# One partition maximum for the keys of all images, behind the last image

## What is computed

```python
xf = x.reshape(b, n, d)
keys = xf @ Wk.T
softmax_keys = jax.nn.softmax(keys, axis=1)
values = _bn(xf @ Wv.T, gamma_v, beta_v, axes=(0, 2), ch_shape=(1, -1, 1))
queries = _bn(queries, gamma_q, beta_q, axes=(0, 2, 3), ch_shape=(1, -1, 1, 1))
content_lambda = jnp.einsum('bmk,bmv->bkv', softmax_keys, values)
position_lambdas = jnp.einsum('nmk,bmv->bnkv', E, values)
content_output = jnp.einsum('bknh,bkv->bhvn', queries, content_lambda)
position_output = jnp.einsum('bknh,bnkv->bhvn', queries, position_lambdas)
return (content_output + position_output).reshape(b, d, n1, n2)
```

## Time and profile before

| | |
|---|---|
| median of 3 runs | 1595.41 us (1594.87 to 1595.89) |
| profiled execution | 1599.93 us, span 1598.2 us |
| TensorE busy | 1483.3 us, 93% of the span |
| VectorE busy | 1016.7 us, 64% |
| GpSimd busy | 675.6 us, 42% |
| ScalarE busy | 427.5 us, 27% |

### The profile page before, as it was taken

One profiled execution on the slowest core, in us unless ns is written; L12 is line 12 of the kernel. 1 busy time (PEld: TensorE's weight loads), 2 busy tenths in 40 slices (PEclk: granted clock), 3 DMA queues, 4 the chain that ended last, 5 costly groups with the idle time before them and its releaser, 6 DMA issues.

```text
span 1598.2 us, 27819 instructions
## 1 busy us (share of the span) xinstructions
PE 1483.3 (93%) x10407; PEld 1243.3 (78%) x10407; DVE 1016.7 (64%) x1496; ACT 427.5 (27%) x738; POOL 675.6 (42%) x453
## 2 busy tenths in 40 slices
PE   6765368999999999999999999999999999999997
PEld 6655247888888888888888888888888888888886
DVE  6645597666666666666666666666666666666663
ACT  4435432222222222222222222222222222222220
POOL 4333525444444444444444444444444444444441
PEclk9878689999999999999999999999999999999999
DMA  6453142233343434241525243333434251525221
GB/s 227 170 192 112 15 65 60 60 90 68 74 85 85 85 85 86 60 92 45 112 59 112 59 103 67 78 67 85 85 85 85 76 95 47 92 58 112 59 52 27
DMA packets 338460, 134.68 MB, mean 84 GB/s; under 512 B 202640, under 2 KB 333824, under 8 KB 337920
## 3 DMA queue, kind: packets, MB, share of 16 engines
q1 hardware_dynamic: 338432, 134.31, 36.7%
HBM read 109.12 MB, written 25.17 MB: 84 GB/s over the span
## 4 chain that ended last, share of the span: by engine, by line
PE 87%; issue 5%; DVE 3%; POOL 3%; ACT 1%; DMA 0%; DVEq 0%; SPq 0%; POOLq 0%; ACTq 0%
PE ps_a L989 76%; PE ps_b L1008 8%; PE ps_b L919 2%; POOL x_in L398 1%; PE ps_a L909 1%; POOL keys L405 1%; DVE e_lo L679 1%; POOL key_top L403 0%; DVE b_lo L691 0%; DVE bn L639 0%; PE ps_b L950 0%; DVE q_stats L671 0%; DMA x_in<-in_x 0%; DVE t_lo L691 0%; ACT x_t L500 0%
## 5 line engine op out<-in xcount | busy, mean ns | idle before, releaser
L989 PE MATMUL ps_a<-v_hi,e_hi 128*128 128x512 f32 x1792 | 706.0, 394 | 12.8 <-issue 12.1
L989 PE MATMUL ps_a<-v_hi,e_lo 128*128 128x512 f32 x1792 | 699.0, 390 | 0.0
L989 PEld LDWEIGHTS ps_a<-v_hi,e_hi 128*128 128x128 f32 x1792 | 337.1, 188 | 86.6 <-issue 12.9
L989 PE MATMUL ps_a<-b_lo,e_hi 128*128 128x512 f32 x1024 | 399.2, 390 | 2.6 <-DVE b_lo L691 2.6
L989 PEld LDWEIGHTS ps_a<-v_hi,e_lo 128*128 128x128 f32 x1792 | 337.3, 188 | 68.2
L525 ACT ACTIVATE e_hi<-e_nat 128x512 fp32r<-128x512 f32 x320 | 202.1, 632 | 603.4 <-PE ps_a L989 598.3
L437 POOL TENSOR_TENSOR q_diag<-qn,row_mask 128x1024 f32<-128x1024 f32 x128 | 249.1, 1967 | 222.4 <-PE ps_b L1008 208.2
L433 POOL TENSOR_TENSOR e_nat<-e_nat,s_buf 128x512 f32<-128x512 f32 x64 | 83.5, 1305 | 553.3 <-DVE e_lo L679 553.3
L679 DVE TENSOR_TENSOR e_lo<-e_nat,e_hi 128x512 fp32r<-128x512 f32 x320 | 301.1, 941 | 2.0 <-ACT e_hi L525 0.3
L989 PE MATMUL ps_a<-t_lo,e_hi 128*128 128x512 f32 x768 | 300.0, 391 | 0.0
L752 DVE TENSOR_TENSOR pos<-ps_a,content 128x512 f32<-128x512 f32 x189 | 130.7, 692 | 178.4 <-PE ps_a L989 175.9
(11 more groups left out here) (107 smaller groups left out, 758.5 us busy)
## 6 DMA issues: line engine op xcount, KB each, us to landing
e_nat<-in_L_conv_E SPq DMA_DIRECT2D x128, 512.0 KB, 4.8
x_in<-in_x SPq DMA_DIRECT2D x32, 512.0 KB, 4.2
res<-in_x SPq DMA_DIRECT2D x64, 256.0 KB, 6.8
out_dram<-res SPq DMA_DIRECT2D x64, 256.0 KB, 4.9
q_dram<-q_nat SPq DMA_DIRECT2D x4, 2048.0 KB, 7.6
q_blk<-q_dram SPq DMA_DIRECT2D x32, 256.0 KB, 5.4
gam_q<-in_L_conv_gamma_q SPq DMA_DIRECT2D x8, 0.1 KB, 4.9
bet_q<-in_L_conv_beta_q SPq DMA_DIRECT2D x8, 0.1 KB, 4.6
```

Source lines behind the costliest of these rows:

```text
L989: ins = nc.tensor.matmul(BANK_OF[i], e[:, i, j].rearrange("p n k -> p (n k)"), v[:, j], start=(STARTS[i] and j == 0 and n == 0), stop=(STO ...
```

## The change

key_max and key_top become four times as large and hold all quarters. The buffers move to regions that are free at that time (over content and q_blk), so SyncE waits for keys_shifted before it loads q_blk. keys_max(a) no longer waits for the subtraction, only for the one before it of its own kind. GpSimd does one maximum over 512 columns, when all four key_max are there, and then four subtractions, four exponentials are done by ScalarE, and four sums by GpSimd. e_sums moves ahead of the maximum.

```diff
@@ buffers
         top_level = sb("top_level", [P, J // 2, G, KD], stack=early)
+        key_top = sb("key_top", [P, A, G, KD], stack=early)
...
         v_stats = sb("v_stats", [P, J, A, 6], stack=early)
+        key_max = sb("key_max", [P, A, G, KD], stack=early)
...
-        key_max = sb("key_max", [P, G, KD], stack=early)
-        key_top = sb("key_top", [P, G, KD], stack=early)
@@ SyncE
             sp.wait_ge(v_var_ready, 1)
+            sp.wait_ge(keys_shifted, 1)
             load_q(0, 0)
             load_q(1, 1)
@@ GpSimd
+            def reduce_keys():
+                pool.wait_ge(key_max_ready, A)
+                link(pool.partition_all_reduce(key_top[:].rearrange("p a g k -> p (a g k)"),
+                                               key_max[:].rearrange("p a g k -> p (a g k)"), P, RMAX))
+
             def shift_keys(a):
-                pool.wait_ge(key_max_ready, a + 1)
-                link(pool.partition_all_reduce(key_top[:].rearrange("p g k -> p (g k)"),
-                                               key_max[:].rearrange("p g k -> p (g k)"), P, RMAX))
-                pool.tensor_tensor(keys[:, :, :, a], keys[:, :, :, a], key_top[:].unsqueeze(1).to_broadcast([P, J, G, KD]),
+                pool.tensor_tensor(keys[:, :, :, a], keys[:, :, :, a], key_top[:, a].unsqueeze(1).to_broadcast([P, J, G, KD]),
                                    ALU.subtract).then_inc(keys_shifted, 1)
...
             for k in range(len(BATCHES)):
                 norm_images(k)
-                if k == 4:
-                    shift_keys(0)
-                if k == 6:
-                    shift_keys(1)
+            e_sums(0, 0, 32, first=True)
+            reduce_keys()
+            for a in range(A):
+                shift_keys(a)
             sum_keys(0)
-            e_sums(0, 0, 32, first=True)
-            shift_keys(2)
             sum_keys(1)
-            shift_keys(3)
@@ ScalarE
                 read_proj(8 * a + G - 1, a, G - 1, a % QS)
-                if a == 2:
-                    exp_keys(0)
-                if a == 3:
-                    exp_keys(1)
-                    exp_keys(2)
-
...
-            exp_keys(3)
+            for a in range(A):
+                exp_keys(a)
             value_split_hi(0)
@@ VectorE
             def keys_max(a):
                 dve.wait_ge(proj_read, 8 * a + 8)
                 if a > 0:
-                    dve.wait_ge(keys_shifted, a)
+                    dve.wait_ge(key_max_ready, a)
...
-                nc.vector.tensor_tensor(key_max[:], top_level[:, 0], top_level[:, 1], ALU.max).then_inc(key_max_ready, 1)
+                nc.vector.tensor_tensor(key_max[:, a], top_level[:, 0], top_level[:, 1], ALU.max).then_inc(key_max_ready, 1)
```

## The result

The changed kernel takes 1556.78 us (median of 4 runs, 1556.22 to 1557.45), against 1595.65 for the kernel before in the same comparison (4 runs, 1594.87 to 1597.36). The ratio is 0.9755, 95% interval 0.9738 to 0.9772. That is 38.9 us less, where 34.7 was forecast, and inside the range of 1551 to 1574. The profiled execution took 1557.23 us for a span of 1555.5, which is 42.7 us less than the profiled one before. The two differences disagree by 3.8 us, because the profiled execution of before (1599.93) was 4.3 us above the median of this comparison, and this one is 0.45 above its own. In every comparison the executions of the kernel before spread from about 1595 to 1600; what parts them was not found.

The account below looks back on a forecast made before the run. The opening was taken as a serial path whose last wait at each place is GpSimd. 35.5 + 10.4 - 10.2 - 1.0 = 34.7 us, so 1595.4 becomes 1560.7 us; the range holding 8 in 10 is 1551 to 1574.

Parts of the forecast that it names:

- Part 1: Between the images: without two partition maxima the last gn_bias comes at 96.6 instead of 132.1, a gain of 35.5 us.
- Part 2: Last gn_bias to last key maximum: VectorE's 8.78 us wait goes and its maxima take 1.4 us, a gain of 10.4 us.
- Part 3: Last key maximum to last subtraction: three more subtractions (6.9 us) and a longer partition maximum (3.3 us), a loss of 10.2 us.
- The forecast's signs for this part: After the last key maximum, M: the partition maximum's record some 6 us later, the first subtraction at about M + 21.3.
- The growth by the columns: Extra time of one partition maximum of 512 columns over one of 128: 3.3 us, between bounds 0 and 6.6.
- Part 4: Behind the last subtraction: all four sums of exponentials, then L461, come later; price 1 us, bounds -1.5 and +5.
- the 19 forecast: The sums of exponentials on GpSimd are ready near 19 us behind the last subtraction.
- (C): Opening: images don't keep the pace as loads, stores and statistics meet; 16 us a group, 9 us more, 1570; chance 6%.
- (A): Partition maximum grows with its columns at 4.94 us: growth 14.8 instead of 3.3, 1572.2 us; chance 8%.
- (D): Slower than before: the long maximum's cost per column eats the gain, from 0.099 us a column; chance 3%.
- (B): Serial tail: sums of quarters 0 and 1 and L461 land on the path, 9.9 us instead of 1.0, 1569.6; chance 8%.

Follow-up runs that it names:

- spread statistics: The changed kernel with VectorE's statistics spread evenly between the groups of images, some moved behind the last group: 1553.61 us, ratio 0.973.
- kernel with the fill: The changed kernel with a fill of one element per partition, waiting for the last key maximum, put directly ahead of the partition maximum: 1564.04 us, ratio 0.9787.
- doubled maximum: The changed kernel with its partition maximum of 512 columns done twice in a row, same input and output: 1559.6 us, ratio 0.9757.
- kernels without a maximum: The changed kernel with the partition maximum replaced by an ordinary GpSimd fill of key_top with zeros, subtractions kept: 1553.94 us, ratio 0.9725.
- VectorE's subtractions: The changed kernel with the four key subtractions on VectorE, behind its normalisation of the values, instead of on GpSimd: 1553.54 us, ratio 0.9718.

## Why the prediction was right

The sign, the place and the range were right: 34.7 us against 38.9 in the medians and 42.7 in the profiles. That the sum came so near is partly luck, since one of its four steps failed and another was too large. By its own steps, which are counted in the profiles:

- **Part 1**, 35.5 us: measured 31.8 (132.06 to 100.24). The mechanism holds, and the size was off by 3.7. One gap of four images was 13.1 as taken, but the first took 14.0 (59.06 to 73.05), and the last 14.05 instead of 11.2. The step took 13.1 and 11.2 from gaps that have neither of two things, and a gap of 14.0 has both (11.2 + 1.6 + 1.2). The first is the clock: after a wait of 1.90 us for VectorE, the eight transposes of the next image take 1.95 us instead of 1.07 and its projection 2.69 instead of 1.94; the granted clock is 0.60 from 57 to 60 us, so most of it went at the lower of the clock's two levels, 1.2 GHz in place of 2.4. The same kernel, run again, has the same wait of 1.90 us at 57.53 and a granted clock of 1.00 behind it, and that gap is 12.7 us (59.09 to 71.76); so the fall doesn't come every time. The second is TensorE's wait of 1.18 us for ScalarE's copy at the turn of a quarter, which stands in both gaps of 14.0. So in the last gap VectorE's lateness, the only thing the step took off, wasn't the bound: VectorE waited 6.40 us for the average there. In before both lay in the gaps with the maxima, which the step replaced whole. The spread statistics, which take away the wait for VectorE, got the last gn_bias 6.0 us sooner.
- **Part 2**, 10.4 us: measured 132.23 to 163.88 against 100.40 to 121.61, a gain of 10.4. The maxima took 1.4 us, as taken.
- **Part 3**, a loss of 10.2 us: measured none. From the last key maximum to the end of the last subtraction it is 20.2 us before and after (121.61 to 141.80). This is the step that failed: it says that "the same stretch has the same VectorE work beside it" and takes over the 5.97 us until the record and the 4.94 us in it. The 5.97 us were read as a cost that stands behind M; they begin where GpSimd's last sum ends (163.74), 0.14 us ahead of M, so the row couldn't tell which of the two set the start. But the loading starts as soon as GpSimd has nothing ordinary left to do, ahead of the wait, and then the maximum is over before VectorE's long two-input operations begin (123.56 against 127.63). Each is shown: with the loading held back (the kernel with the fill), both come back and the first subtraction moves from 9.0 to 19.1 us behind the last key maximum. The forecast's signs for this part failed: the record follows 0.14 us behind M, not some 6, and the first subtraction 9.0 us behind it, not 21.3. So 5.7 us of loading and 3.1 us of the record went (1.81 instead of 4.94), and the subtractions cost 8.8 us more (11.15 instead of 2.31), which comes to nothing. The growth by the columns, 3.3 us in the sum, was 1.1, shown by the doubled maximum. The rule of the Trainium skill (Perfetto Trace Analysis, GPSIMD Engine Instruction) to go by spacings of starts gives the same as the record if two maxima in a row are taken (1.91 us against 1.80). What misled was the spacing to the next ordinary instruction, which contains the loading back. The four subtractions took 11.15 us instead of 9.2, since the first met VectorE's last t_raw (130.44 to 132.73).
- **Part 4**, a loss of 1 us: measured 25.2 instead of 24.3 us to the first evacuation, 0.9. The size is right, but partly by chance. VectorE lost less than I thought, since its last operation came ahead of L461. The sums were ready 17.9 us behind the last subtraction (159.69), even before the 19 forecast, but TensorE, having waited 7.92 us, did the small sums and the first product at the low clock (0.58 granted from 161 to 168 us): 7.2 us from 159.75 to the evacuation, where the two took 3.9 in before. That didn't fit into the slack, and held the evacuation by 1.99 us. The stretch behind it gives back 1.6 us (43.0 at the first query product against 41.4 at the first evacuation): in before VectorE waited 1.80 us for the second product, which ran at 0.64 of the clock, and now it waits 0.22, with 1.00 granted.

The sum of the measured steps is 31.8 + 10.4 + 0.0 - 0.9 + 1.6 = 42.9, against 42.7 in the spans. So two errors, +3.7 and -10.2, went against each other, and the profiled execution of before, a long one, makes the gain in the profiles 3.8 us larger than in the medians. Two terms on record are added up wrongly, without weight for the forecast: by the records the growth is at most 2.2, so 1.1 us under the 3.3 taken and not 2, and 16 us a group (C) would come to 10.6 us more, not 9.

Of the rivals, (A) and (D) are excluded by the record and by the doubled maximum: 0.003 us for each added column, (1.81 - 0.72) / 384. The estimate of 0.121 us a column from the Trainium skill (GPSIMD Engine Reference, Cross-partition — where GPSIMD wins) is some 40 times that. The page gives its figure for tensor_reduce, and this kernel uses another instruction; no run here shows the page's. (C) is excluded by the gaps of 13 to 14 us. (B) was right about the mechanism and wrong about the price in this kernel: TensorE waited 7.92 us for the sums, and 0.9 arrived. It decides what comes next, as the kernels without a maximum and with VectorE's subtractions show, which gained 9 us ahead of it and kept 3.

## What to carry to other kernels

Count an instruction of a loaded GpSimd library by its switches: batch such instructions, so that they share a loading and a loading back, and leave GpSimd idle ahead of them, with no ordinary instruction that waits for the same input in between. Then the first loading costs nothing. When such a term goes, ask at once which second path ends next, and look at the two-input operations of VectorE and GpSimd in the same stretch: whoever comes second there waits until the other's instruction has ended, so an operation that was short in its old place needn't be so in its new one.

## What the runs showed of the hardware

- A switch of the GpSimd library took 5.8 to 6.0 us until the library's instruction began, and 6.8 to 7.6 us from its end to the next ordinary one, behind the images. Beside the transfers of images it took 6.9 to 7.8 and 7.7 to 10.3. The loading begins ahead of the semaphore wait of the instruction that needs it (109.7 against 121.61).
- Library instructions in a row need one loading: four maxima took 5.15 us together, and one pair of configurations stands ahead of them.
- The partition maximum took 0.72 us for 128 columns and 1.81 for 512, alone; 4.94 and 5.79 beside VectorE operations with two SBUF operands.
- When an operation of VectorE with two SBUF operands meets one of GpSimd, the second waits for the end of the first: t_lo took 6.62 us instead of 2.28 beside GpSimd's L461 (159.31 to 164.29), and a split of 0.69 us took 4.42.
- VectorE's batch-norm statistics, with one SBUF operand, keep their length beside GpSimd's subtractions: 32 of them took 10.52 us there (the subtractions ran until 136.51), and 10.53 in the changed kernel, in a stretch without them (at 106.00). That doesn't hold for every operation with one large operand: VectorE's six normalisations of the values took 13.92 us beside the subtractions, against 4.46.
- After the same wait of 1.90 us, TensorE's granted clock fell in one execution of the changed kernel (0.60 from 57 to 60 us) and stayed at 1.00 in another.
